# Cross-attention on one core: the context's normalisation and the batch's last body rescheduled, the last key sums inverted in 16 columns

## The chip, the core and the metric

One core of a Trainium2 chip. The metric is the device time of one execution in microseconds; lower is better. Everything is float32; products are made from a high part in `fp32r` and a low remainder, so that each product takes three matmuls (high x high, high x low, low x high).

## What is computed

Eight batches of 512 queries `x` and 512 context rows, width 1024, 16 heads of 64:

```python
a = layer_norm(ctx, gamma, beta)
Q, K, V = x @ Wq.T, a @ Wk.T, a @ Wv.T          # split into 16 heads
scores = where(mask, Q @ K.T / 8, -inf)
out = (softmax(scores) @ V) @ Wo.T
return x + tanh(gate) * out
```

## The kernel before

**Bodies.** Each batch `b` has eight bodies `j`, one for a pair of heads: 64 bodies `k = 8 b + j`. Body `k` makes the scores of pair `k`, the projections Q, K and V of pair `k + 1` (a `stream` of 72 matmuls of 512 columns, handed out in portions by `take`), the products of the probabilities with V, and the output projection of pair `k - 2`. A body's `kind` is "plain", "prepare" (`j` = 6, which also transposes the next batch's normalised context, `turn_ctx`) or "switch" (`j` = 7, whose projections are the first to read the next batch's `x` and context). The last body, 63, is written out by itself.

**Queues.** Each engine runs its own list in the order written, and semaphores join them; there is no planner. TensorE's order is `body` with the portions in `FILL`. For each head of a pair the scores go to PSUM (`sc`), VectorE takes maxima (L790, L796), ScalarE and VectorE pass them across partitions (`gather_maxima` L581, `key_maxima` L802, `hand_out_maxima` L586, `spread_maxima` L807), VectorE subtracts (L812), ScalarE does `exp` (L601) and the high part `p_high` (L606), GpSimd the low part `p_low` (L1055), and TensorE multiplies with V (`values`, L377 and L378). GpSimd also adds up the probabilities (`key_sums`, L1059 and L1061), scales the output of the pair before (`o_scale`, L1066) and makes its low part (L1070).

**Between bodies.** `copy_vt` (L591) is the first thing ScalarE does in a body. It copies the V just projected out of PSUM; the bank it frees takes the next Q projection, so that projection waits for it (`vt_done`). `q_high`, `q_low` (L612, L840), `k_high` and `k_low` (L619, L845) split the projected Q and K; the next body's scores wait for them, and the V projection, which uses Q's bank, waits for `q_low`.

**The context of the next batch** is loaded in bodies 1 to 3. VectorE takes statistics of half rows (`row_stats`, L895) in bodies 2 to 5. In body 5 it joins them (`row_moments`), ScalarE makes variance plus epsilon and the negated mean (`moments`, L629), GpSimd the reciprocal deviation (L1074) and then normalises four blocks of 128x1024 (`norm_rows`, L1078). In body 6 TensorE transposes, and ScalarE applies gamma and beta (`a_float`, L661), two blocks at a time, eight in all. At the end of body 6 ScalarE makes the high parts of the first four blocks (`a_high`, L670), at the start of body 7, behind `copy_vt`, those of the other four; GpSimd makes the low parts (`a_low`, L1089) in body 7. `x_high` (L657) and `x_low` do the same for `x` in body 6; block 0 stands before `gather_maxima`. The rows that carry the mask in the key operand are written at the end of body 7 (`mask_rows`, L638).

**The first batch** splits the weights as well: ScalarE `split_w` (L576) and GpSimd (L1050), up to four of 128x1024 in each body; SyncE loads them to `w_raw` and stores the parts in HBM (`keep_w`) for the other batches (`load_kept`).

**The last body.** The sums of exponentials come from matmuls with ones (L497, L498), which leave the same sum in all rows, 512 columns. VectorE inverts 64x512 for each head (`inverse_rows`, L957), scales the last pair's output (L949), ScalarE makes its high part `last_hi` (L645), VectorE the low part (L953). The output projections of pairs 62 (`before_pair`) and 63 (`last_pair`) are added in PSUM; VectorE adds them to `xy` (`gather`, L962), and SyncE stores.

## Time and profile before

| what | us |
|---|---|
| median of 3 runs | 2028.72 (2027.18 to 2029.65) |
| profiled execution, its own time | 2029.85 |
| its span, first to last instruction | 2028.0 |
| mean granted TensorE clock | 0.995 of full |

The page gives one line of busy times for the engines; in the timelines each line is an instruction or several alike: start, duration (of all of them together), engine, line, operation, tiles, count, and in brackets the idle time before it and what ended it. The end of a matmul is modelled, so a 512-column matmul shows about 0.39 us though the next starts 0.23 us after it; an idle time in brackets counts from the modelled end and is about 0.16 us shorter than the time that was lost.

### The profile page before, as it was taken

The page shows a single profiled execution, that of the slowest core. Times are in us where ns is not written, and L with a number is a line of the kernel's source. Part 1 is how long each engine was busy: PE and PEld are TensorE (multiplying, and loading weights), DVE is VectorE, ACT ScalarE, POOL GpSimd, SP SyncE. Part 2 cuts the span into 40 slices and gives each one's busy share as a digit, 9 for nine tenths or more (in the row PEclk, how much of TensorE's full clock was granted, in tenths as well). Part 3 has the DMA queues.
Part 4 walks back from the last instruction along what each step waited for, and adds up shares of the span by engine and source line. Part 5 has one row for each costly group of instructions (what it writes and reads, how often), then busy time and mean ns, then how long its engine had stood idle before and what let it go on. Part 6 is the DMA issues. An engine that isn't in the chain of part 4 may idle for free.

```text
span 2028.0 us, 26183 instructions
## 1 busy us (share of the span) xinstructions
PE 1957.3 (97%) x8720; PEld 1590.0 (78%) x8720; DVE 1617.7 (80%) x2074; ACT 1282.3 (63%) x2362; POOL 1501.9 (74%) x831
## 2 busy tenths in 40 slices
PE   5899989999999999999999999999999999999997
PEld 4688768888788877888778887788778888788885
DVE  6688667887778877888778887788877888787887
ACT  5767766567656585656865657665675566755563
POOL 5899996769865788667876678666886668857663
PEclk9999999999999999999999999999999999999998
DMA  6577544653355443554345553454433644434422
GB/s 243 187 249 251 181 155 158 223 185 137 126 185 194 169 167 106 211 202 144 136 149 189 189 187 108 148 211 167 167 124 135 246 157 157 146 123 174 168 93 97
DMA packets 136501, 341.95 MB, mean 169 GB/s; under 512 B 55856, under 2 KB 56880, under 8 KB 135472
## 3 DMA queue, kind: packets, MB, share of 16 engines
q1 hardware_dynamic: 136368, 340.28, 47.6%
q8 instruction: 70, 1.15, 0.2%
q14 instruction: 63, 0.52, 0.1%
HBM read 288.86 MB, written 51.36 MB: 168 GB/s over the span
## 4 chain that ended last, share of the span: by engine, by line
PE 78%; POOL 9%; ACT 5%; DVE 4%; issue 2%; DMA 2%; SPq 1%; ACTq 0%; DVEq 0%; POOLq 0%
PE pj L433 14%; PE pj L437 14%; PE pj L435 14%; PE sc L383 5%; PE sc L387 5%; PE sc L384 5%; PE sc L359 5%; PE pv L377 5%; PE sc L360 5%; PE pv L378 5%; POOL a_lo L1089 4%; POOL p_lo L1055 2%; DVE mq L790 1%; PE pj L366 1%; DMA xy<-in_xT 1%
## 5 line engine op out<-in xcount | busy, mean ns | idle before, releaser
L1055 POOL TENSOR_TENSOR p_lo<-prob,p_hi 128x1024 fp32r<-128x1024 f32 x256 | 613.5, 2407 | 185.7 <-ACT p_hi L606 185.6
L433 PE MATMUL pj<-a_hi,w_hi 128*128 128x512 f32 x1024 | 403.3, 394 | 5.9 <-DVE v_st L834 2.3
L437 PE MATMUL pj<-a_hi,w_lo 128*128 128x512 f32 x1024 | 401.2, 392 | 0.0
L435 PE MATMUL pj<-a_lo,w_hi 128*128 128x512 f32 x1024 | 400.8, 391 | 0.0
L790 DVE TRANSPOSE_TENSOR_REDUCE mq<-sc 128x32 f32<-128x1024 f32 x256 | 304.6, 1228 | 100.3 <-PE sc L360 99.3
L857 DVE SCALAR_TENSOR_TENSOR xy<-sc,tg_b,xy 128x1024 f32<-128x1024 f32 x244 | 306.1, 1273 | 44.0 <-PE sc L387 38.1
L601 ACT ACTIVATE prob<-prob 128x1024 f32<-128x1024 f32 x256 | 271.6, 1061 | 109.6 <-DVE prob L812 109.3
L812 DVE TENSOR_TENSOR prob<-sc,m_b 128x1024 f32<-128x1024 f32 x256 | 301.6, 1220 | 4.4
L1059 POOL TENSOR_TENSOR prob<-prob 128x1024 f32<-128x1024 f32 x126 | 302.4, 2400 | 0.0
L606 ACT CAST p_hi<-prob 128x1024 fp32r<-128x1024 f32 x256 | 269.4, 1052 | 3.5
L1066 POOL TENSOR_TENSOR r_b<-o,r_b 128x512 f32<-128x512 f32 x62 | 80.9, 1304 | 242.0 <-DVE r_b L829 242.0
L433 PEld LDWEIGHTS pj<-a_hi,w_hi 128*128 128x128 f32 x1024 | 193.0, 188 | 50.8 <-POOL a_lo L1089 5.1
L437 PEld LDWEIGHTS pj<-a_hi,w_lo 128*128 128x128 f32 x1024 | 193.0, 188 | 41.6
L435 PEld LDWEIGHTS pj<-a_lo,w_hi 128*128 128x128 f32 x1024 | 193.1, 189 | 41.0
L612 ACT CAST qt<-pj 64x512 fp32r<-64x512 f32 x128 | 74.4, 581 | 233.2 <-PE sc L360 208.5
L377 PE MATMUL pv<-p_hi,v_st 128*128 128x512 f32 x512 | 201.0, 393 | 19.2 <-POOL p_lo L1055 19.2
L433 PE MATMUL pj<-x_hi,w_hi 128*128 128x512 f32 x512 | 208.2, 407 | 5.7 <-issue 4.4
L359 PE MATMUL sc<-qt,kt 128*128 128x512 f32 x512 | 201.4, 393 | 12.6 <-ACT cx L661 4.9
L435 PE MATMUL pj<-x_lo,w_hi 128*128 128x512 f32 x512 | 202.2, 395 | 0.0
L437 PE MATMUL pj<-x_hi,w_lo 128*128 128x512 f32 x512 | 201.4, 393 | 0.0
L378 PE MATMUL pv<-p_lo,v_st 128*128 128x512 f32 x512 | 200.2, 391 | 0.0
L360 PE MATMUL sc<-qt,kt 128*128 128x512 f32 x512 | 200.1, 391 | 0.0
(122 smaller groups left out, 3700.2 us busy)
## 6 DMA issues: line engine op xcount, KB each, us to landing
w_hi<-kept_hi SPq DMA_DIRECT2D x225, 512.0 KB, 3.7
w_lo<-kept_lo SPq DMA_DIRECT2D x225, 512.0 KB, 4.6
cx<-in_ctx SPq DMA_DIRECT2D x32, 512.0 KB, 6.5
xy<-in_xT SPq DMA_DIRECT2D x32, 512.0 KB, 6.3
kept_hi<-w_hi SPq DMA_DIRECT2D x32, 512.0 KB, 5.3
kept_lo<-w_lo SPq DMA_DIRECT2D x32, 512.0 KB, 6.1
out_y<-xy SPq DMA_DIRECT2D x7, 2048.0 KB, 9.8
w_raw<-in_wq SPq DMA_DIRECT2D x8, 512.0 KB, 5.3
```

The costliest lines, as they stand in the source:

```text
L359: pe.matmul(sc[:, s], kt[:, h, 0, cols], qt[:, h, 0], start=True, stop=False)
L360: mm = pe.matmul(sc[:, s], kt[:, h, 1, cols], qt[:, h, 1], start=False, stop=True)
L377: pe.matmul(pv[h][:, 0], w, p_hi[:, s], start=s == 0, stop=False)
L378: mm = pe.matmul(pv[h][:, 0], w, p_lo[:, s], start=False, stop=s == TB - 1)
L433: pe.matmul(dst, w_hi[:, w, cols], s_hi[:, i], start=i == 0, stop=False)
L435: pe.matmul(dst, w_hi[:, w, cols], s_lo[:, i], start=False, stop=False)
L437: mm = pe.matmul(dst, w_lo[:, w, cols], s_hi[:, i], start=False, stop=i == KT - 1)
L790: dve.tensor_reduce(out=mq[:, 2 * i:2 * i + 2], in_=sc[:, 2 * i:2 * i + 2].rearrange("p s (b j) -> p s b j", j=32), op=ALU.max, axis=mybir ...
L812: dve.tensor_tensor(prob[:, h, 2 * i:2 * i + 2], sc[:, 2 * i:2 * i + 2], m_b[:].rearrange("p (o t) -> p o t", o=1).to_broadcast((P, 2, T)) ...
L857: dve.scalar_tensor_tensor(out=y, in0=sc[:, 2 * where:2 * where + 2], scalar=tg_b[:, bass.ds(parity, 1)], in1=y, op0=ALU.mult, op1=ALU.add ...
L1055: pool.tensor_tensor(p_lo[:, 2 * i:2 * i + 2], prob[:, h, 2 * i:2 * i + 2], f32(p_hi[:, 2 * i:2 * i + 2]), ALU.subtract).then_inc(pl_done, 1)
L1059: pool.tensor_tensor(prob[:, h, 0:2], prob[:, h, 0:2], prob[:, h, 2:4], ALU.add).then_inc(sum_done, 1)
```

## The change

- Row statistics are regrouped, and joined in two pairs: blocks 0 and 1 in body 4, blocks 2 and 3 in body 5 (`MOMENTS`). GpSimd makes the reciprocal deviations of a pair behind `key_sums(k, 0)`.
- The normalisation itself goes from GpSimd to ScalarE, in quarters of two passes each, an addition of the negated mean and a product (`norm_quarter`): behind `hand_out_maxima` of the second head in bodies 4 and 5, and before `gather_maxima` of the first head in bodies 5 and 6 (`NORM`).
- In body 6 all `x_high` of the first half stand behind `hand_out_maxima(k, 0)`. In body 7 the first four `a_high` stand behind `copy_vt` and `o_high`, the other four behind `hand_out_maxima(k, 0)`, and `mask_rows` behind `hand_out_maxima(k, 1)`.
- TensorE, body 7, second head: the nine matmuls that followed the second half of `values` now precede it (`late`).
- SyncE, body 7 of the first batch: the load of the last weight block, and the stores of the one before, stand further ahead.
- Last body: each sum is reduced with transposition to 16 columns (`row_sums`), inverted there and spread by one transposition (`last_inverse`). One `gather` moves behind the last low part, and `before_pair(1)` behind the first two `last_pair`.

The start of the kernel calls the changed helpers with b = -1 and does the same work as before. The diff, cut:

```diff
...
 CTX_LOADS = {1: (0, 1), 2: (2,), 3: (3,)}
-ROW_STATS = {(2, 1): (0,), (3, 0): (1,), (3, 1): (2,), (4, 0): (3, 4), (4, 1): (5,), (5, 0): (6, 7)}
-MASK_BODY, NORM_BODY = 2, 5
+ROW_STATS = {(2, 1): (0,), (3, 0): (1, 2), (3, 1): (3,), (4, 0): (4,), (4, 1): (5,), (5, 0): (6, 7)}
+
+MOMENTS = {(4, 0): 0, (5, 0): 1}
+NORM = {(4, 1): 0, (5, 0): 1, (5, 1): 2, (6, 0): 3}
+MASK_BODY = 2
...
                 k = PAIRS - 1
+                sp.wait_ge(wlo_done, NUMBER[WO, k - 2] + 1)
+                sp.dma_start(w_raw[:, NUMBER[WO, k - 1] % 2], wts[WO][k - 1]).then_inc(w_ld[NUMBER[WO, k - 1] % 2], 16)
                 sp.wait_ge(w_out[WV], 32 * PAIRS)
                 load_kept(WV, 0, k)
+                keep_w(NUMBER[WO, k - 2])
                 exchange_sums(k - 1)
...
                 load_kept(WK, 1, k)
-                sp.wait_ge(wlo_done, NUMBER[WO, k - 2] + 1)
-                sp.dma_start(w_raw[:, NUMBER[WO, k - 1] % 2], wts[WO][k - 1]).then_inc(w_ld[NUMBER[WO, k - 1] % 2], 16)
-                keep_w(NUMBER[WO, k - 2])
                 sp.wait_ge(wlo_done, SPLITS)
...
                         values(*before, 0)
-                    take(stream, f[1])
+                    late = f[2] if kind == "switch" and h else 0
+                    take(stream, f[1] + late)
                     if started:
...
                         turn_v(k)
-                    take(stream, f[2])
+                    take(stream, f[2] - late)
                     out_step(k, h, 0, kind)
...
                 before_pair(0, upper)
-                pe.wait_ge(pinv_done, 1)
+                pe.wait_ge(prow_done, 1)
                 before_pair(2, pj_both)
-                pe.wait_ge(acc_done, 4 * k - 4)
-                before_pair(1, lower)
                 pe.wait_ge(w_in_last, 32)
...
                 last_pair(2, pj_both)
+                pe.wait_ge(acc_done, 4 * k - 4)
+                before_pair(1, lower)
                 last_pair(1, lower)
...
-            def moments(b):
-                act.wait_ge(bn_done, b * 3 * TB + 6 * TB)
-                act.activation(vpe[:], mv[:, :, 1], ACT.Identity, bias=eps[:]).then_inc(stat_done, 1)
-                act.mul(nmean[:], mv[:, :, 0], -1.0).then_inc(stat_done, 1)
+            def moments(b, pair):
+                rows = slice(0, TB) if b < 0 else slice(2 * pair, 2 * pair + 2)
+                act.wait_ge(bn_done, b * 3 * TB + (6 * TB if b < 0 or pair else 4 * TB + 3))
+                act.activation(vpe[:, rows], mv[:, rows, 1], ACT.Identity, bias=eps[:]).then_inc(stat_done, 1)
+                act.mul(nmean[:, rows], mv[:, rows, 0], -1.0).then_inc(stat_done, 1)
+
+            def norm_quarter(b, s):
+                act.wait_ge(stat_done, b * 4 + 4 + 2 * (s // 2))
+                act.activation(cx[:, s], cx[:, s], ACT.Identity, bias=nmean[:, s:s + 1]).then_inc(centre_done, 1)
+                act.wait_ge(rstd_done, b * 2 + 2 + s // 2)
+                act.wait_ge(centre_done, b * TB + s + 1)
+                act.mul(cx[:, s], cx[:, s], rstd[:, s:s + 1]).then_inc(z_done, 1)
...
                     o_high(k - 2)
-                if kind == "prepare":
-                    x_high(k, b, 0, (b + 1) % 2)
+                if (j, 0) in NORM and b < B - 1:
+                    norm_quarter(b, NORM[j, 0])
+                if kind == "switch":
+                    for i in range(KT // 2):
+                        a_high(k, b, i)
+                gather_maxima(k, 0)
+                hand_out_maxima(k, 0)
                 if kind == "switch":
...
                         a_high(k, b, i)
-                gather_maxima(k, 0)
-                hand_out_maxima(k, 0)
                 split_w(b, WV, j + 1)
                 if kind == "prepare":
-                    for i in range(1, KT // 2):
+                    for i in range(KT // 2):
                         x_high(k, b, i, (b + 1) % 2)
...
                 q_high(k, 1)
-                if j == NORM_BODY and b < B - 1:
-                    moments(b)
+                if (j, 0) in MOMENTS and b < B - 1:
+                    moments(b, MOMENTS[j, 0])
                 gather_maxima(k, 1)
                 hand_out_maxima(k, 1)
+                if kind == "switch":
+                    mask_rows(k, b)
+                if (j, 1) in NORM and b < B - 1:
+                    norm_quarter(b, NORM[j, 1])
                 split_w(b, WQ, j + 2)
...
                     a_float(b, 7)
-                    for i in range(KT // 2):
-                        a_high(k + 1, b, i)
-                if kind == "switch":
-                    mask_rows(k, b)
                 if splits(b, WO, j - 1):
...
             act.wait_ge(eps_done, 1)
-            moments(-1)
+            moments(-1, 0)
             for i in range(KT):
...
-            def row_moments(b):
-                dve.wait_ge(bn_done, b * 3 * TB + 5 * TB)
-                dve.nop(nofuse=True)
-                for s in range(TB):
+            def row_moments(b, pair):
+                dve.wait_ge(bn_done, b * 3 * TB + (3 * TB + 2 * TB if b < 0 else 4 * TB + pair * (TB + 2)))
+                for s in range(TB) if b < 0 else (2 * pair, 2 * pair + 1):
                     dve.bn_aggr(mv[:, s], bn[:, s].rearrange("p a c -> p (a c)")).then_inc(bn_done, 1)
...
                     row_stats(b, i)
-                if stats and j == NORM_BODY:
-                    row_moments(b)
+                if stats and (j, 0) in MOMENTS:
+                    row_moments(b, MOMENTS[j, 0])
                 if stats and j == MASK_BODY:
...
-            def inverse_rows(h, sums):
+            def row_sums(h, sums):
                 dve.wait_ge(psum_done, 2 * h + 2)
-                dve.reciprocal(last_r[halves[h]], sums[halves[h]]).then_inc(pinv_done, 1)
+                dve.tensor_reduce(out=mq[:, h], in_=sums.rearrange("p (b j) -> p b j", j=32), op=ALU.max,
+                                  axis=mybir.AxisListType.X, apply_transpose=True).then_inc(prow_done, 1)
+
+            def last_inverse():
+                for h in range(2):
+                    dve.wait_ge(prow_done, h + 1)
+                    dve.reciprocal(r_inv[halves[h]], mq[halves[h], h]).then_inc(pinv_done, 1)
+                dve.wait_ge(pinv_done, 2)
+                dve.transpose(last_r.rearrange("p (b i) -> p b i", i=32),
+                              r_inv[:].rearrange("p (b o) -> p b o", o=1).to_broadcast((P, 16, 32))).then_inc(pinv_done, 1)
...
                 gather(4 * k - 5, upper, 2)
-                inverse_rows(0, pj[0])
-                gather(4 * k - 4, lower, 3)
+                row_sums(0, pj[0])
                 o_add(k, 1, last_o)
-                inverse_rows(1, pv[0][:, 0])
-                dve.wait_ge(pinv_done, 2)
+                row_sums(1, pv[0][:, 0])
+                last_inverse()
+                dve.wait_ge(pinv_done, 3)
                 dve.wait_ge(oadd_done, k * 2 + 2)
...
                 low(k, last_lo, last_r, last_hi)
+                gather(4 * k - 4, lower, 3)
                 gather(4 * k - 3, upper, 0)
...
                 row_stats(-1, i)
-            row_moments(-1)
+            row_moments(-1, 0)
             dve.wait_ge(rstd_done, 1)
...
-            def norm_rows(b, blocks=range(TB)):
-                pool.wait_ge(stat_done, b * 2 + 4)
-                pool.tensor_tensor(rstd[:], vpe[:], nhalf[:], ALU.pow).then_inc(rstd_done, 1)
-                pool.wait_ge(rstd_done, b + 2)
-                pool.nop(nofuse=True)
-                for s in blocks:
+            def deviations(b, pair):
+                rows = slice(0, TB) if b < 0 else slice(2 * pair, 2 * pair + 2)
+                pool.wait_ge(stat_done, 2 if b < 0 else b * 4 + 4 + 2 * pair)
+                pool.tensor_tensor(rstd[:, rows], vpe[:, rows], nhalf[:, rows], ALU.pow).then_inc(rstd_done, 1)
+
+            def first_norm():
+                pool.wait_ge(rstd_done, 1)
+                for s in range(2, TB):
                     pool.tensor_scalar(cx[:, s], cx[:, s], nmean[:, s:s + 1], rstd[:, s:s + 1], ALU.add,
...
                 key_sums(k, 0)
+                if (j, 0) in MOMENTS and b < B - 1:
+                    deviations(b, MOMENTS[j, 0])
                 split_w(b, WQ, j + 2)
...
                 split_w(b, WK, j + 2)
-                if j == NORM_BODY and b < B - 1:
-                    norm_rows(b)
                 if begun:
...
             split_w(0, WQ, 0)
-            norm_rows(-1, range(2, TB))
+            deviations(-1, 0)
+            first_norm()
             for i in range(KT // 2, KT):
...
```

## Rows read from the trace of the kernel before

**Rows 1.** The page, part 1: engine, busy us (share of the span) xinstructions.

```profile
PE 1957.3 (97%) x8720; PEld 1590.0 (78%) x8720; DVE 1617.7 (80%) x2074; ACT 1282.3 (63%) x2362; POOL 1501.9 (74%) x831
```

**Rows 2.** Who waited for whom, TensorE: total us, times, longest us.

```profile
PE pv L377 <- POOL p_lo L1055: 19.2, 11, 3.4
```

**Rows 3.** Timeline, ScalarE: start us, us, operation [idle before <-releaser], bodies 29 to 32.

```profile
937.47 0.59 ACT L591 COPY vt<-pj 128x512 f32<-128x512 f32 x1 [1.00 <-PE pj L437]
...
967.17 0.59 ACT L591 COPY vt<-pj 128x512 f32<-128x512 f32 x1 [1.00 <-PE pj L437]
...
1002.94 0.59 ACT L591 COPY vt<-pj 128x512 f32<-128x512 f32 x1
...
1034.11 0.59 ACT L591 COPY vt<-pj 128x512 f32<-128x512 f32 x1 [0.76 <-PE pj L437]
```

**Rows 4.** Timeline, TensorE, the switch body of the fourth batch.

```profile
1001.03 0.50 PE L359 MATMUL sc<-qt,kt 128*128 128x512 f32 x1 [0.62 <-ACT cx L661]
...
1003.62 0.47 PE L433 MATMUL pj<-x_hi,w_hi 128*128 128x512 f32 x1 [0.49 <-issue]
...
1009.91 0.50 PE L383 MATMUL sc<-o_hi,w_hi 128*128 128x512 f32 x1
...
1023.91 0.50 PE L377 MATMUL pv<-p_hi,v_st 128*128 128x512 f32 x1 [1.63 <-POOL p_lo L1055]
```

**Rows 5.** Timeline, ScalarE and VectorE, around the start of that body.

```profile
1000.87 2.17 ACT L670 CAST a_hi<-cx 128x512 fp32r<-128x512 f32 x4
...
1006.15 0.66 ACT L581 COPY m_four<-m_four 32x16 f32<-32x16 f32 x3
...
1004.67 0.27 DVE L796 TENSOR_REDUCE m_four<-mq 128x16 f32<-128x64 f32 x1
```

**Rows 6.** Timeline, GpSimd and VectorE, the same body.

```profile
1021.49 2.37 POOL L1055 TENSOR_TENSOR p_lo<-prob,p_hi 128x1024 fp32r<-128x1024 f32 x1
...
1022.23 0.69 DVE L840 TENSOR_TENSOR qt<-pj,qt 64x512 fp32r<-64x512 f32 x1
```

**Rows 7.** Timeline, ScalarE, bodies 28 and 29 (plain).

```profile
930.24 1.06 ACT L601 ACTIVATE prob<-prob 128x1024 f32<-128x1024 f32 x1 [1.14 <-DVE prob L812]
...
941.09 0.66 ACT L581 COPY m_four<-m_four 32x16 f32<-32x16 f32 x3 [2.51 <-DVE m_four L796]
```

**Rows 8.** Timeline, ScalarE, start of body 46 (sixth batch).

```profile
1461.62 0.62 ACT L657 CAST x_hi<-xy 128x512 fp32r<-128x512 f32 x1 [3.12 <-DMA xy<-in_xT]
```

**Rows 9.** Timeline, ScalarE, start of body 5 (first batch).

```profile
188.87 0.59 ACT L591 COPY vt<-pj 128x512 f32<-128x512 f32 x1
```

**Rows 10.** Timeline, GpSimd, body 5 (first batch).

```profile
216.03 4.75 POOL L1078 TENSOR_SCALAR cx<-cx,nmean,rstd 128x1024 f32<-128x1024 f32 x4 [0.18 <-POOL rstd L1074]
```

**Rows 11.** Timeline, TensorE, bodies 6, 7 and 8 (first batch).

```profile
224.49 0.65 PE L377 MATMUL pv<-p_hi,v_st 128*128 128x512 f32 x1 [3.37 <-POOL p_lo L1055]
...
285.16 0.50 PE L377 MATMUL pv<-p_hi,v_st 128*128 128x512 f32 x1 [2.60 <-POOL p_lo L1055]
...
300.10 0.47 PE L433 MATMUL pj<-x_hi,w_hi 128*128 128x512 f32 x1 [1.38 <-ACT vt L591]
```

**Rows 12.** Windows: stretch, length, busy by engine (PE first), then PEclk, DMA share, GB/s.

```profile
224.50:228.50 4.00, 4.00 (x11) 3.15 (x12) 2.42 (x5) 1.97 (x7) 4.00 (x2) 0.57 0.03 11
285.00:289.50 4.50, 4.34 (x12) 3.44 (x13) 1.17 (x4) 2.95 (x5) 4.42 (x4) 0.62 0.13 40
2014.50:2020.00 5.50, 5.44 (x13) 4.28 (x14) 1.93 (x2) 0.00 (x0) 0.00 (x0) 0.50 0.06 25
```

**Rows 13.** Timeline, VectorE and TensorE, the last body.

```profile
1997.36 0.25 DVE L826 RECIPROCAL r_inv<-r_sum 128x16 f32<-128x16 f32 x1
...
1997.65 0.71 DVE L829 STREAM_TRANSPOSE r_b<-r_inv 128x512 f32<-128x512 f32 x1
...
2004.60 3.34 DVE L957 RECIPROCAL w_raw<-pj 64x512 f32<-64x512 f32 x1
...
2014.56 0.77 PE L383 MATMUL sc<-x_hi,w_hi 128*128 128x512 f32 x1 [3.56 <-ACT x_hi L645]
```

3 lines of the change are left out of this document (2 added, 1 removed).

## The prediction

> **What bounds the kernel now.** Read the page's part 1 first: TensorE is busy 97% of the span, the other engines 63 to 80% [rows 1]. So a change here can only win back stretches in which TensorE waits or runs at half clock, and it loses wherever it makes another engine late for TensorE. The waits of TensorE come next: the longest entry is the products with V (L377) waiting for the low parts of the probabilities from GpSimd, 19.2 us [rows 2]. Then find where they lie. ScalarE copies the new V out of PSUM once in each body, as soon as TensorE has finished it, so the starts of L591 are a ruler for bodies: the plain body 29 takes 967.17 - 937.47 = 29.70 us; body 30, which also transposes the context, 35.77; body 31, the batch's last, 31.17 [rows 3]. Body 31 has a plain body's matmuls, and both of its neighbours wait, so the loss sits at the turn of each batch. Everything else that can be won is in the first batch and behind the last body's scores.
>
> **The turn of a batch, six times (batches 2 to 7).** In body 31 TensorE stops four times; each wait is the start in its row less the expected start, one matmul (0.23 us, from 29.70 us for 128 matmuls of 512 columns and a short transposition) after the one before [rows 4]:
> (a) 1001.03, 0.78 us, for the last `a_float` of ScalarE. The change does not touch the chain before it: it stays.
> (b) 1003.62, 0.64 us, for `copy_vt`, which stands behind four `a_high` (2.17 us) [rows 5]. They go behind it: the copy starts at 1000.95, is out by 1001.55, ahead of the end of the scores (1002.98). Gone.
> (c) 1009.91, 0.27 us, for the first subtraction. Four more `a_high` behind the copy, as long again, kept `gather_maxima` back until 1006.15, though VectorE's maxima were there at 1004.67 + 0.27 [rows 5]. Now only the first four lie there, 1001.95 to 1004.1. The subtraction comes 1.2 us earlier, TensorE 0.64. Gone.
> (d) 1023.91, 1.78 us, for `p_low(k, 0, 1)`, which GpSimd ended at 1023.86 after working without a break since `o_low` [rows 6]. `o_high` now runs at 1001.4 instead of 1003.4, so GpSimd starts its row 2.0 us earlier and ends it at 21.9; and `late` puts nine matmuls, 2.1 us, before these products, which TensorE reaches at 1023.91 - 1.78 - 0.91 + 2.1 = 1023.3. Gone with 1.4 us to spare.
> What is late next: the nine matmuls hold six of the V projection, which may start only when `q_low` (L840) of the second head is done, 1022.91 before [rows 6], 0.91 earlier now, so 1022.0 against TensorE at 1021.9: 0.15 us lost. `o_move(k, 0)` waits for the postponed products, so ScalarE's second half ends 0.9 us later against TensorE than in a plain body; `k_low` still ends about 0.1 us ahead of the next scores: I take nothing, at most 0.3. The mask rows (two passes, 1.5 us) fall into the wait of `o_move`, 2.3 us long, and free the end of the body. The second four `a_high` move 2.7 us later, to 1008.8; GpSimd needs the fifth at about 1012.
> Gain 0.64 + 0.27 + 1.78 - 0.15 = 2.5, and some 0.2 because the matmuls after a wait are issued slightly apart: **2.7 us, 2.2 to 3.0; times six 16.2**.
>
> **The context's normalisation on ScalarE.** A quarter is two passes over 128x1024. ScalarE's pass of that size costs 1.06 [rows 7], two dependent ones 2.1. Body 28 (quarter 0) and 29 (quarter 2) put it behind `hand_out_maxima(k, 1)`: there `o_move` (0.6) and a wait of 1.14 stand before `exp` [rows 7], which then starts 0.45 late; the chain behind it ends 1.0 us before the next V copy [rows 3], so this is covered. The wait for `rstd` costs nothing there: GpSimd makes it while the maxima are passed round. Quarter 1 lies in the gap of 2.51 us before `gather_maxima` in body 29 [rows 7], quarter 3 in the same gap of body 30, which `x_high(0)` leaves. If a pass were 1.3 us (a bias and a scale from columns), the slots overrun by up to 0.1 us each: 0 to 0.3 per batch. GpSimd's saved time in these batches is worth nothing, it has slack. Quarter 3 must be done before the transposes, 5 us later. Moving `x_high(0)` gives one thing more: in body 46 it waited 3.12 us for a transfer, with the maxima behind it [rows 8], and that body was 1.2 us longer than its like: **1.2** (0 to 1.2, as arrival varies). The row statistics are only regrouped; two in one slot were there before.
>
> **The first batch** differs, since the weights are split there as well. ScalarE has no idle time left in bodies 4 and 5: the copy of V starts at 188.87 with no wait noted [rows 9], where elsewhere it waits 1.00 for V [rows 3]. The quarter (2.1) and the wait for `rstd` behind GpSimd's sums (0.4) push `k_high` and the copy back 2.5 us; slack 0.65; TensorE loses 1.9 twice, and 0.5 where the subtraction is late: -4.3. GpSimd no longer spends 4.75 us on four normalisations [rows 10], but 1 us more on a second `rstd`, and twice waits 2.1 us for the splits: it leaves body 5 0.9 us earlier. The wait of 3.37 us at 224.49 goes [rows 11], and with it the stretch behind it with granted clock 0.57, mostly the lower level of 1.2 GHz [rows 12], eight matmuls at 0.43 instead of 0.23: +5.1. Net 0.8.
> Body 7: GpSimd works without a pause and holds TensorE. Its `a_lo` undo what (b) and (c) give, but the wait of 2.60 us [rows 11] takes in nine matmuls (2.1), and the half-clock run behind it (1.6) goes. At the end the copy of V waited for a weight split that waited for transfers: 1.38 and 0.2 of issue [rows 11]. The load of that weight and the two stores of the one before now stand ahead of the exchange of sums: gone. On SyncE the load's wait for `wlo_done` (GpSimd, 265.5) holds back the load of V's weights and all behind it by some 7 us; TensorE wants them at about 282: covered. Sum 0.8 + 2.1 + 1.6 + 1.5 = **6.0, bounds 2 and 10**.
>
> **The last body.** VectorE inverts the key sums of each head in 64x512, 3.34 us for the first [rows 13] and as much for the second, with a gather (1.2) between. The new way reduces each to 16 columns: the trace has no such pass from PSUM; bounds 0.61 (half of L790's 1228 ns) and 1.2; I take 0.70, the transposition of 128x512 being 0.71 [rows 13]. Then two inversions of 0.25, a transposition of 0.71 [rows 13], and 0.4 of semaphore steps: removed 7.9, added 2.9. The last high part and TensorE's restart move from 2014.56 to 2009.5. Before, 30 matmuls followed, the first 12 at 0.43 (granted clock 0.50 [rows 12]): 9.5 us. Now 36 follow, since `before_pair(1)` has moved behind; at full clock 36 x 0.23 + 0.3 for the low part = 8.5. **5.06 + 1.0, take 5.9**; without the full clock 3.5.
> This hangs on TensorE's wait there, now about 1.3 us instead of 3.56 [rows 13]. Here the wait of 1.63 left the clock full (the matmul took 0.50 [rows 4], those at half clock 0.65 and 0.77 [rows 11, 13]); after the one of 2.60 the granted clock fell to 0.62 [rows 12]. [...]
>
> **How the numbers follow.** 16.2 + 1.2 + 6.0 + 5.9 = 29.3 us. The profiled execution took 2029.85 (span 2028.0), less 29.3 is 2000.55; the median, 2028.72, gives **1999.4**. With all terms at their good ends it is 1993, at their bad ends 2010; as these don't meet, 1994.5 to 2006.5. Chance 0.78.
> Rival A: the first batch gives nothing, as ScalarE's extra 2.5 us per body also delays splits and loads, and the clock falls in the tail: 1999.4 + 6.0 + 2.4 = 2008. For it: ScalarE is full there; against: GpSimd's 4.75 us are surely freed. 0.12.
> Rival B: at each turn a new wait takes the place of (d), for `q_low` or `k_low`, which have 0.1 us: only (b) and (c) stay, 6 x 1.8 less: 2010. 0.06.
> Rival C, slower: a ScalarE pass with a column operand costs as much as GpSimd's p_lo, 2.37 [rows 6]. A quarter is then 4.8, 2.7 more; three slots overrun by 2.1, the fourth by 2.3, 8.6 per batch, seven batches: +60 - 29 = 2059. Break-even at 4.2 per batch, a pass of 1.8 us. Against it 1.06 in [rows 7]. By the Trainium skill, ScalarE: Activation LUTs, What ACT_TABLE_LOAD costs, such a pass is some 0.28 us + 0.833 ns per element, 1.13 us: an estimate that speaks for the forecast. The page's rules for authors want additions and products on VectorE; no run shows it here. 0.02.
> Rival D: the waits removed come back elsewhere, no change: 2028. 0.02.
> The range of 1994.5 to 2006.5 leaves the rivals out. Differences under 0.2% (4 us) can't be told from no change. Faster 0.96, same 0.02, slower 0.02.
>
> **What would show it.** Starts of L591: body 30, 35.8 before, about 33.8, since the copy starts 2 us earlier; body 31, 31.2 before, about 30.4; together 64.2 instead of 66.9. No wait before L377 in a switch body, the one before L359 unchanged. Passes on cx near 1.06 us. In the first batch new TensorE waits of about 1.9 at the ends of bodies 4 and 5, none of 3.4. In the tail the last matmul about 14 us after the first inversion starts, formerly 19. The prediction is wrong if plain bodies 4 and 5 exceed 29.8 in later batches, or if V's projection waits over 0.5 us for `q_low`.

## The result and the profile after

The changed kernel takes 2005.09 us (median of 4 runs, 2002.27 to 2006.49) against 2029.18 for the kernel before (median of 4): ratio 0.9881, 95% interval 0.9864 to 0.9898. That is 24 us faster; 1999.4 was forecast. Its profiled execution is its fastest, 2002.27 (span 2000.5); by the spans it is 27.5 us faster than the profiled one of the kernel before.

The page, part 1, after:

```profile
PE 1950.9 (98%) x8720; PEld 1585.3 (79%) x8720; DVE 1614.8 (81%) x2077; ACT 1343.3 (67%) x2432; POOL 1472.9 (74%) x810
```

TensorE executes the same 8720 matmuls and still bounds the kernel. 61 us of busy time have come to ScalarE and 29 have left GpSimd [rows 1]. The waits of TensorE after, in the form of [rows 2]:

```profile
PE sc L363 <- DVE kt L861: 7.3, 4, 2.1
PE sc L363 <- ACT cx L674: 5.0, 7, 1.2
PE pv L381 <- POOL p_lo L1080: 3.5, 3, 1.4
PE pj L437 <- POOL a_lo L1116: 2.4, 7, 0.5
```

The products with V wait 3.5 us for GpSimd instead of 19.2. In front now stand the scores behind `k_low` (two of the four waits are at the start, two at the ends of the first batch's bodies 4 and 5) and, seven times, the scores of the switch body behind the last `a_float`.

The ruler of the prediction, ScalarE's copies of V at the starts of bodies 29 to 32, as in [rows 3]:

```profile
925.17 0.59 ACT L596 COPY vt<-pj 128x512 f32<-128x512 f32 x1 [0.27 <-PE pj L441]
...
955.11 0.59 ACT L596 COPY vt<-pj 128x512 f32<-128x512 f32 x1 [0.27 <-PE pj L441]
...
988.86 0.58 ACT L596 COPY vt<-pj 128x512 f32<-128x512 f32 x1
...
1019.41 0.59 ACT L596 COPY vt<-pj 128x512 f32<-128x512 f32 x1 [0.21 <-PE pj L441]
```

Body 30 takes 33.75, body 31 30.55, together 64.30; 33.8, 30.4 and 64.2 were forecast. But body 29 takes 29.94 and not 29.70, and the idle time before the copy has shrunk from 1.00 to 0.27.

The same ruler laid over the whole span (differences of starts of the V copy; "first batch" is from the copy of body 4 to that of body 8):

| stretch | before | after | gain | forecast |
|---|---|---|---|---|
| start to body 4 | 159.17 | 157.55 | 1.6 | 0 |
| first batch, bodies 4 and 5 | 59.40 | 63.97 | -4.6 | -4.3 |
| first batch, bodies 6 and 7 | 80.80 | 69.78 | 11.0 | 10.3 |
| batches 2 to 7, bodies 6 and 7 | 402.88 | 386.57 | 16.3 | 17.4 |
| batches 2 to 7, bodies 0 to 5 | 1068.41 | 1071.20 | -2.8 | 0 |
| batch 8, bodies 56 to 62 | 207.90 | 207.98 | -0.1 | 0 |
| last body | 49.44 | 43.45 | 6.0 | 5.9 |
| sum | 2028.0 | 2000.5 | 27.5 | 29.3 |

### The profile page after: what moved, and what is told of

The parts are those of the page before. It is cut to its first block, busy times and chain, and to the rows that moved or that the text cites. A ratio compares the mean times of both kernels' runs of the same rounds, so it can differ in the third digit from the quotient of the medians.

```text
span 2000.5 us, 26247 instructions
## 1 busy us (share of the span) xinstructions
PE 1950.9 (98%) x8720; PEld 1585.3 (79%) x8720; DVE 1614.8 (81%) x2077; ACT 1343.3 (67%) x2432; POOL 1472.9 (74%) x810
## 3 DMA queue, kind: packets, MB, share of 16 engines
q8 instruction: 70, 1.15, 0.2%
## 4 chain that ended last, share of the span: by engine, by line
PE 83%; ACT 6%; DVE 6%; POOL 2%; issue 2%; DMA 1%; SPq 0%; ACTq 0%; DVEq 0%; POOLq 0%
PE pj L437 15%; PE pj L441 15%; PE pj L439 15%; PE sc L387 5%; PE sc L363 5%; PE sc L391 5%; PE sc L364 5%; PE sc L388 5%; PE pv L381 5%; PE pv L382 5%; DVE mq L806 2%; PE pj L370 1%; ACT prob L606 1%; ACT cx L674 1%; ACT x_hi L670 1%
```

## Experiments

The kernels are the changed one with one edit each, unless another base is named; segments are read with the same ruler. The kernel before took 2030.4 us beside the first four, 2029.8 beside the next four and 2029.2 beside the last three.

**The changed kernel again.** No edit.

> The changed kernel itself, looked at again. Its profiled execution spans 2000.5 us and has granted clock 0.999, while other executions took 2 to 4 us more at 0.997. Theory: these differ in how many of TensorE's waits of 2 to 2.3 us (bodies 0 to 2) and 1.3 us (last body) are followed by some eight matmuls at 0.43 instead of 0.23 us, 1.6 us for each such stretch; this profile then shows such stretches and a clock below 0.999 where its span is above 2001, and the same waits to 0.1 us. Rival: transfers arrive later in the slower executions; then the clock is 0.999 and new waits for DMA appear. Median about 2004 us, ratio to before 0.988.

Measured: 2004.79 us, ratio 0.9873 (0.9857 to 0.9889); its profiled span is 2002.3. Segment by segment it is within 0.5 us of the other profile but for one: bodies 0 to 3 take 115.34 and not 113.39. TensorE there in this run, with its window from 53 to 60 us (columns as in [rows 12]):

```profile
53.38 0.47 PE L437 MATMUL pj<-a_hi,w_hi 128*128 128x512 f32 x1 [2.04 <-DVE v_st L850]
...
54.06 0.63 PE L441 MATMUL pj<-a_hi,w_lo 128*128 128x512 f32 x1
```

The window:

```profile
53.00:60.00 7.00, 6.62 (x22) 5.31 (x23) 2.00 (x3) 3.62 (x6) 6.47 (x3) 0.76 0.75 245
```

The same in the first profile of the changed kernel:

```profile
53.44 0.47 PE L437 MATMUL pj<-a_hi,w_hi 128*128 128x512 f32 x1 [2.04 <-DVE v_st L850]
...
53.97 0.40 PE L441 MATMUL pj<-a_hi,w_lo 128*128 128x512 f32 x1
```

The window:

```profile
53.00:60.00 7.00, 6.57 (x29) 5.46 (x30) 3.56 (x5) 4.74 (x7) 6.41 (x3) 1.00 0.71 246
```

The wait is the same, 2.04 us. Behind it one execution ran eight matmuls at 0.43 us (1.2 GHz; granted clock of the window 0.76) and the other ran them at 0.23 (2.4 GHz; 1.00): 22 matmuls against 29 in the window. The DMA share is alike. So the 1.6 us that the table shows ahead of body 4 are the clock: the profile of before shows the fall, that of after does not, and the change has no part in it. All thirteen profiles of this document agree: the time to body 4 is 157.6 to 158.7 us where TensorE runs no stretch of matmuls at 0.43 ahead of it, 158.9 to 159.6 with one such stretch and 160.4 to 161.0 with two. New waits for transfers, as the rival had it, do not appear. The gain of the change itself, profile against profile, is about 26 us.

**The tail alone.** The kernel before, with `row_sums`, `last_inverse` and the new order of the last products only.

```diff
...
-                inverse_rows(0, pj[0])
-                gather(4 * k - 4, lower, 3)
+                row_sums(0, pj[0])
                 o_add(k, 1, last_o)
-                inverse_rows(1, pv[0][:, 0])
-                dve.wait_ge(pinv_done, 2)
+                row_sums(1, pv[0][:, 0])
+                last_inverse()
...
```

> The kernel before with the new last body alone (row_sums, last_inverse, the moved gather and before_pair). Theory: the time from the V copy of body 63 to the end goes from 49.4 to 43.4 us, all else stays: 6.0 us less, about 2023 us. Rival: half of it was the half-clock stretch behind the wait of 3.56 us, which the new wait of 1.3 us calls forth as well; then 3.5 us less, about 2025.5, with a stretch of 0.43 us per matmul behind the last high part.

Measured: 2025.27 us, ratio 0.9973 (0.9961 to 0.9984). The last body takes 43.36 instead of 49.44, all other segments but the start are within 0.8 us of before. TensorE, and the window behind its restart:

```profile
2010.77 0.47 PE L384 MATMUL sc<-x_hi,w_hi 128*128 128x512 f32 x1 [1.32 <-ACT x_hi L646]
```

The window:

```profile
2010.50:2016.00 5.50, 5.24 (x22) 4.13 (x23) 4.46 (x4) 0.12 (x1) 0.00 (x0) 1.00 0.22 91
```

The wait is 1.32 in place of 3.56 [rows 13], and 22 matmuls start in the 5.5 us in which 13 did [rows 12], at a granted clock of 1.00 instead of 0.50. The term of 5.9 us stands by itself: 6.1. The median is 5.1 below that of the kernel before and lies where the rival had it, but the rival needed a stretch at half clock behind the last high part, and there is none.

**The normalisation back on GpSimd.** Everything else of the change stays, the reciprocal deviations in pairs too; `norm_quarter` goes, and in body 5 GpSimd normalises the four blocks.

```diff
-                if (j, 0) in NORM and b < B - 1:
-                    norm_quarter(b, NORM[j, 0])
...
-                if (j, 1) in NORM and b < B - 1:
-                    norm_quarter(b, NORM[j, 1])
...
                 split_w(b, WK, j + 2)
+                if j == 5 and b < B - 1:
+                    norm_rows(b)
```

> The changed kernel with the four normalisations back on GpSimd in body 5, moments still in two pairs, everything else as changed. Theory: the move to ScalarE is worth little, since what GpSimd gains in the first batch (wait of 3.4 us and a half-clock stretch, 5 us) ScalarE loses there (waits of 1.68, 0.42, 1.68 and 0.44 at 188, 197, 220 and 229 us) and 0.2 to 0.4 us in each later batch: within 2.5 us of the changed kernel, bodies 4 and 5 at 29.7 us, body 6 at 40 to 42. Rival: GpSimd was the late engine and the move is the main gain outside the last body: 5 us or more slower than changed, spread over all batches.

Measured: 2004.38 us, ratio 0.9869 (0.9854 to 0.9884), span 2001.3: the change as it is gives no more. GpSimd and TensorE in the first batch:

```profile
215.30 4.80 POOL L1104 TENSOR_SCALAR cx<-cx,nmean,rstd 128x1024 f32<-128x1024 f32 x4
...
223.83 0.47 PE L381 MATMUL pv<-p_hi,v_st 128*128 128x512 f32 x1 [2.25 <-POOL p_lo L1076]
```

Bodies 4 and 5 are back at 29.73 and 29.71 (31.94 and 32.03 with the quarters), bodies 6 and 7 take 39.30 and 35.12 (36.38 and 33.40). Without the quarters the first batch wins 4.5 and loses 4.6. In the later batches body 5 is 29.70 again and not 29.94. The 39.30 of body 6 hold, behind the wait of 2.25 shown, eight matmuls at 0.43 us, 1.6 us, which another execution may lack. So the move of the normalisation, the largest part of the diff, is worth nothing in the places that the change gives it; the gain is that of the order of ScalarE's and TensorE's work at the turn, the load order and the tail.

**Without `late`.** TensorE's nine matmuls again follow the products with V.

```diff
-                    late = f[2] if kind == "switch" and h else 0
+                    late = 0
```

> The changed kernel with late = 0. Theory: in a switch body TensorE asks for p_low(k, 0, 1) at about 1009.0 and has it at 1009.85: 0.8 us lost instead of the 0.27 for q_low, so 0.5 to 0.6 us more in each of six batches, and in the first batch the wait before L381 becomes about 2.3 us, possibly with a half-clock stretch: 3 to 4 us. Total 5 to 7 us slower than changed. Rival: the postponed products delay o_move and with it k_low by as much as they save: no difference (under 1.5 us).

Measured: 2010.28 us, ratio 0.9898, by the medians 5.2 to 5.5 more than the changed kernel. The span, 2008.2, is 7.7 longer than its first profile's, but 2.9 of these lie ahead of body 4, where this execution has two stretches of matmuls at 0.43 us and that one none. The largest wait for a low part is back in body 7:

```profile
285.26 0.50 PE L381 MATMUL pv<-p_hi,v_st 128*128 128x512 f32 x1 [2.59 <-POOL p_lo L1080]
```

The first batch's body 7 is 1.3 longer (34.71), and each later batch 0.3 to 1.3. In the fourth batch the same wait reads:

```profile
1015.68 0.50 PE L381 MATMUL pv<-p_hi,v_st 128*128 128x512 f32 x1 [0.70 <-POOL p_lo L1080]
```

Here TensorE loses 0.86 of the 1.78 us of (d) [rows 4]: the earlier order on ScalarE alone removes 0.92, and `late` the rest. The next run has `late` without that order, and no wait for `p_low` in its switch bodies either, so `late` alone would have removed all of it. The wait of 2.59 at 285.26 was followed by no stretch at half clock here (granted clock 1.00 from 285 to 290), that of 2.60 before the change was [rows 12].

**`a_high` in its old places.** Four `a_high` ahead of `copy_vt` again, and the other four ahead of `gather_maxima`.

```diff
-                    for i in range(KT // 2):
+                    for i in range(KT // 2, KT):
                         a_high(k, b, i)
                 gather_maxima(k, 0)
                 hand_out_maxima(k, 0)
-                if kind == "switch":
-                    for i in range(KT // 2, KT):
-                        a_high(k, b, i)
...
                     a_float(b, 7)
+                    for i in range(KT // 2):
+                        a_high(k + 1, b, i)
```

> The changed kernel with the first four a_high back at the end of body 6 and the other four back ahead of gather_maxima; mask rows, late and the rest as changed. Theory: the waits of 0.64 (V copy) and 0.27 us (first subtraction) return in six batches, GpSimd starts o_low 2 us later and is then 1.2 us late for nothing, as late covers it: 0.9 to 1.3 us per batch, 6 to 8 us in all; in the first batch GpSimd's a_lo chain hides it. Rival: GpSimd's 2 us push p_low(k, 0, 1) past the cover of late: 2 us or more per batch, 12 us in all, with waits before L381.

Measured: 2012.18 us, ratio 0.9912, span 2010.6. ScalarE and TensorE at the turn of the fourth batch:

```profile
994.14 2.17 ACT L683 CAST a_hi<-cx 128x512 fp32r<-128x512 f32 x4
996.22 0.59 ACT L596 COPY vt<-pj 128x512 f32<-128x512 f32 x1
...
996.90 0.47 PE L437 MATMUL pj<-x_hi,w_hi 128*128 128x512 f32 x1 [0.49 <-issue]
```

The copy of V starts behind the four passes, and TensorE loses 0.65 at 996.90 and 0.25 behind it: (b) and (c) of the prediction, 0.64 and 0.27. Each later batch is 1.0 to 1.2 longer, 6.6 in six; by the medians the kernel is 7.1 to 7.8 slower. The trace names "issue" as the releaser of the first wait; the order of the rows, not the name, tells that it is the copy.

**The old load order on SyncE.** The load of the last weight block, and the stores of the one before, again behind the loads of K's weights.

```diff
-                sp.wait_ge(wlo_done, NUMBER[WO, k - 2] + 1)
-                sp.dma_start(w_raw[:, NUMBER[WO, k - 1] % 2], wts[WO][k - 1]).then_inc(w_ld[NUMBER[WO, k - 1] % 2], 16)
                 sp.wait_ge(w_out[WV], 32 * PAIRS)
                 load_kept(WV, 0, k)
-                keep_w(NUMBER[WO, k - 2])
...
                 load_kept(WK, 1, k)
+                sp.wait_ge(wlo_done, NUMBER[WO, k - 2] + 1)
...
```

> The changed kernel with SyncE's old order in body 7 of the first batch. Theory: the last weight split waits for its stores again and holds the V copy of body 8: 1.5 us more, all of it between bodies 7 and 8. Rival: with body 7 shorter by 3.7 us than before the transfers have less time, and the wait grows to 3 us or more, with a half-clock stretch.

Measured: 2007.97 us (2003.73 to 2009.09), ratio 0.9889. The profiled execution is the slowest of the four, span 2007.3. ScalarE's last weight split waits for the store of the block before; here, and then in the kernel before:

```profile
294.44 1.04 ACT L581 CAST w_hi<-w_raw 128x1024 fp32r<-128x1024 f32 x1 [3.87 <-DMA kept_lo<-w_lo]
...
298.30 1.05 ACT L576 CAST w_hi<-w_raw 128x1024 fp32r<-128x1024 f32 x1 [3.58 <-DMA kept_lo<-w_lo]
```

TensorE behind it, at the end of the first batch, and the window behind:

```profile
296.24 0.77 PE L437 MATMUL pj<-x_hi,w_hi 128*128 128x512 f32 x1 [3.61 <-ACT vt L596]
```

The window:

```profile
296.00:300.00 4.00, 3.76 (x9) 3.02 (x10) 1.85 (x3) 1.82 (x8) 4.00 (x3) 0.50 0.30 120
```

Before, the same wait of TensorE was 1.38 [rows 11]. The split starts 3.9 us earlier than before, but TensorE is there 6.1 us earlier, since body 7 has become shorter: so it waits 3.61, and then runs twelve matmuls at 0.43 us, 2.4 us more. The prediction priced this part at 1.5 us, the size of the wait in the trace of before. In this execution it is worth 6.5: 4.0 up to the V copy of body 8 and 2.5, the half clock, in the batch behind it. By the medians it is worth 2.9 to 3.6, and the fastest execution is no slower than the changed kernel's median. So the size differs between executions, and 6.5 is its upper end; the twelve slow matmuls are one part of it that can be missing. Whether the transfers land at another time was not seen, since one execution was profiled.

**The quarters in other gaps.** The quarters 0 and 2 go from behind `hand_out_maxima(k, 1)` to between `q_high(k, 0)` and `q_high(k, 1)`, where ScalarE waits for the scores of the second head; statistics and deviations half a body earlier.

```diff
+                if (j, 1) in NORM and b < B - 1:
+                    norm_quarter(b, NORM[j, 1])
                 q_high(k, 1)
...
                 hand_out_maxima(k, 1)
...
-                if (j, 1) in NORM and b < B - 1:
-                    norm_quarter(b, NORM[j, 1])
```

> The changed kernel with quarters 0 and 2 moved from behind hand_out_maxima(k, 1) into ScalarE's wait of 3.4 us between q_high(k, 0) and q_high(k, 1); for that the statistics come one step earlier, row_moments stands between group_maxima and key_maxima, moments behind hand_out_maxima(k, 0), and the reciprocal deviations before p_low(k, 0, 0). Theory: ScalarE's fullness behind the second maxima costs the first batch 1.68 + 0.42 + 1.68 + 0.44 us, and GpSimd two waits of 2 us for weight splits; all this goes, and the later batches lose less before k_low (0.1 to 0.3 us each): 5 to 8 us faster than changed, bodies 4 and 5 of the first batch at 29.7 to 30.0 us. Rival: the waits at 188 and 220 us come from the total load of ScalarE, not from the place: bodies 4 and 5 stay above 31 us.

Measured: 1998.18 us, ratio 0.9846 (0.9830 to 0.9863), span 1995.5: 6.6 us below the second run of the changed kernel, 6.2 below the next version, which ran beside it, and 5.0 by the profiles. ScalarE in body 29, and the V copy at the start of body 30:

```profile
934.88 1.16 ACT L640 ACTIVATE cx<-cx,nmean 128x1024 f32<-128x1024 f32 x1
936.12 1.15 ACT L643 ACTIVATE cx<-cx,rstd 128x1024 f32<-128x1024 f32 x1
...
938.27 0.58 ACT L617 CAST qt<-pj 64x512 fp32r<-64x512 f32 x1 [1.00 <-PE sc L364]
...
951.01 0.59 ACT L596 COPY vt<-pj 128x512 f32<-128x512 f32 x1 [0.99 <-PE pj L441]
```

Behind the quarter ScalarE still waits 1.00 for the scores, and before the V copy it waits 0.99, as before the change [rows 3]. In the first batch bodies 4 and 5 take 29.74 and 29.84, and bodies 6 and 7, with GpSimd relieved, keep their 36.35 and 33.44. Against the changed kernel that is 4.4 us in the first batch and up to 0.3 in each other. Against the version with the normalisation on GpSimd it is 4.5 in the first batch and nothing in the others (within 0.1 us each): this is what moving the normalisation can give.

**The tail's last wait filled.** Fourteen more matmuls, whose result is dropped, before the last head's scores, so that TensorE stands idle for less of its longest wait.

```diff
                 turn_v(k)
+                for _ in range(14):
+                    pe.matmul(pj[1], w_hi[:, WK, :P], x_hi[:, 5], start=True, stop=True)
                 scores(k, 1, "last")
```

> The changed kernel with 14 matmuls whose result is dropped in the last body, behind turn_v, where TensorE waits 3.4 us for the first subtraction. Theory: they end before the subtraction does, so nothing is delayed, and the eight matmuls behind the wait run at 0.23 instead of 0.43 us: 1.5 us less between the V copy of body 63 and the end. Rival: the stretch after it is bound by VectorE and GpSimd anyway, as 1.2 and 1.6 us of waits before L381 follow: no gain (under 0.4 us), these waits grow instead.

Measured: 2004.36 us, ratio 0.9873, span 2002.2. The last body takes 43.12 against 43.45 in the first profile of the changed kernel and 43.08 in the second, which had no fall of the clock there either. The own theory had 1.5 us less, the rival under 0.4; the rival held. The version with the quarters in the score wait has the stretch at 0.43 us behind this wait and takes 43.10, so the stretch costs the last body next to nothing.

**The wait for `a_float`, made in the middle of the scores.** Base: the version with the quarters in the score wait. The transposed context lies in the PSUM banks of the third and fourth block of scores, yet TensorE waited for its release ahead of the first.

```diff
-                    if kind == "switch" and h == 0:
-                        pe.wait_ge(at_done, b * KT + 2 * KT)
...
                 for i in range(2):
                     ge(pe, sub_done, k * 4 + 2 * h + i - 1)
+                    if i and floats is not None:
+                        pe.wait_ge(at_done, floats)
```

> On top of the version with the quarters in the score wait (span 1995.5, median 1998.2): in the switch bodies TensorE waits for the last a_float behind the first two blocks of the scores, whose banks hold no transposed context, not ahead of them. Own theory: wait (a) of 0.8 us (0.82 + 0.11 lost at 984.92 there) is only a matter of this order; the first half of the scores takes 0.91 us, so it goes in all seven batches: each batch of the later six 0.7 to 0.9 shorter, 5 us in all, and 0.9 in the first batch; median 1991.5 to 1993.5. Rival: the turn is held by the chain of ScalarE and GpSimd behind it (copy_vt starts only behind the last a_float, GpSimd's low parts end at the same time as before), so the 0.8 us come back within the switch body as waits for the V copy, for p_low(k, 0, 1) or for a_low: batches within 0.2 of before, median 1997 to 1998.5.

Measured: 1993.88 us, ratio 0.9825 (0.9809 to 0.9842), span 1991.3. The later batches are 0.71 to 0.83 shorter each, 4.7 together. The third block's matmul:

```profile
983.90 0.45 PE L365 MATMUL sc<-qt,kt 128*128 128x512 f32 x1
```

It starts 0.22 after the one before, with no wait; the next follows after 0.30. The own theory holds for the later batches, not for the first: body 7 takes 33.48 against 33.44. There the `a_float` comes later still. The wait of 1.36 ahead of the scores is gone, but TensorE loses 0.55 at the third block, 0.38 at the V copy and 0.25 at the first subtraction, as the rival had it; the wait for GpSimd's low part behind them is the same in both, 0.98 and 0.99.

**`q_low` ahead of `key_maxima`.** Same base; VectorE makes `q_low` of the second head while the maxima are gathered, in the switch bodies.

```diff
                 group_maxima(k, 1)
+                if kind == "switch":
+                    q_low(k, 1)
                 key_maxima(k, 1)
-                q_low(k, 1)
+                if kind != "switch":
+                    q_low(k, 1)
```

> On top of the version with the quarters in the score wait: in the switch bodies VectorE makes q_low of the second head before key_maxima, in the 0.79 us in which it waits for the gathered maxima (q_low takes 0.69). Own theory: the V projection's wait for q_low, 0.26 us in six batches and 0.6 in the batch of body 39, goes and nothing takes its place: the switch bodies 0.2 to 0.35 shorter each, median 1996 to 1997. Rival: p_low(k, 0, 1) ends at the same instant (1005.66 against q_low's 1005.67), and key_maxima comes some 0.05 later; TensorE reaches both later parts no earlier, the bodies stay within 0.1: median 1997.5 to 1998.5.

Measured: 1996.88 us, ratio 0.9838 (0.9823 to 0.9853). Its profile has a longer start (the two stretches ahead of body 4 together 2.2 more than its base), so the batches are compared: 0.2 to 0.6 shorter each, 2.3 together (0.6 in the batch of body 39, where a late step of VectorE, told of further on, is gone too); body 31 takes 30.19 instead of 30.56. The own theory holds, with 0.38 per switch body for the 0.26 expected.

**Both edits.**

> Both edits. Own theory: with TensorE 0.8 us earlier in the switch body, q_low and p_low(k, 0, 1) are the next to be late: the products with V come 1.6 us behind the low part without the edits, so 0.5 to 0.8 of it is left, and q_low ahead of key_maxima keeps the V projection free; the gains add up to 1.0 to 1.2 per later batch, median 1989.5 to 1992. Rival: they do not add, since p_low(k, 0, 1) from GpSimd is a bound that neither moves: no better than the first edit alone, within 0.5 us of it.

Measured: 1991.75 us (1990.15 to 1992.71), ratio 0.9813 (0.9799 to 0.9828), span 1988.3. VectorE in the switch body of the fourth batch:

```profile
1000.88 0.69 DVE L856 TENSOR_TENSOR qt<-pj,qt 64x512 fp32r<-64x512 f32 x1
...
1001.65 0.26 DVE L818 TENSOR_REDUCE m_all<-m_four 32x16 f32<-32x64 f32 x1
```

Body 31 takes 29.33, the later batches are 1.1 to 1.5 shorter each than in the base, 7.4 together, where the edits alone gave 4.7 and 2.3. They add up; `p_low(k, 0, 1)`, with its 1.6 us of slack, is not reached. This is the fastest version here, 37 us under the kernel before where the change gave 24.

## Why the prediction was right, and where it was not

**The turn, (a) to (d).** TensorE in the switch body of the fourth batch, after:

```profile
989.01 0.50 PE L363 MATMUL sc<-qt,kt 128*128 128x512 f32 x1 [0.63 <-ACT cx L674]
...
1009.95 0.47 PE L437 MATMUL pj<-a_hi,w_hi 128*128 128x512 f32 x1
```

and VectorE's `q_low` there:

```profile
1009.10 0.69 DVE L856 TENSOR_TENSOR qt<-pj,qt 64x512 fp32r<-64x512 f32 x1
```

(a) stays with 0.79 lost at 989.01; `copy_vt`, the subtraction and `p_low` are no longer waited for; a wait for `q_low` is new at 1009.95. All as forecast, and each tested: (b) and (c) by the old place of `a_high`, (d) by the kernel without `late`, (a) and `q_low` by the last three. Only the size of the new wait was off: 0.27 lost in five batches, where 0.15 was taken, 0.7 us over six. The start of `q_low` had been worked out to 0.1 us on either side, and that it came out so near is in part luck. In body 39 TensorE loses 0.61; the further 0.35 belong to the late step of VectorE below. The two make up the difference between 16.3 and 17.4 in the table.

Body 46, whose transfer was priced at 1.2 us: that wait is gone, and the body now exceeds its like by 0.3, which is again the late step. But the 1.2 was a matter of arrival. In the tail-only run, which has the old order, ScalarE waited 2.28 us for the same transfer and not 3.12, and the body was 0.4 longer than its like, not 1.2.

**The quarters: the step that failed.** That the later start of `exp` in bodies 28 and 29 "is covered" did not hold; the prediction's own sign for it was a plain body 4 or 5 above 29.8 in later batches, and body 5 shows 29.91 to 29.94 (30.29 in one). ScalarE and VectorE at the end of body 28, behind quarter 0, and TensorE in body 29:

```profile
915.92 1.15 ACT L640 ACTIVATE cx<-cx,nmean 128x1024 f32<-128x1024 f32 x1
917.16 1.15 ACT L643 ACTIVATE cx<-cx,rstd 128x1024 f32<-128x1024 f32 x1
...
918.69 1.05 ACT L606 ACTIVATE prob<-prob 128x1024 f32<-128x1024 f32 x1
...
923.86 0.69 DVE L861 TENSOR_TENSOR kt<-pj,kt 64x512 fp32r<-64x512 f32 x1 [0.34 <-ACT kt L625]
...
932.84 0.50 PE L387 MATMUL sc<-o_hi,w_hi 128*128 128x512 f32 x1
```

A pass with an operand per row takes 1.15 to 1.16, not the 1.06 of the passes with a constant scale, and the second starts 1.24 behind the first: the quarter holds ScalarE 2.4 and not 2.1. `exp` starts 2.8 after the handing out of the maxima instead of 2.1, late by 0.7 and not 0.45. That leaves 0.27 of ScalarE's 1.00 before the V copy, so this part is covered; but `k_low` on VectorE waits 0.34 for ScalarE, and all that VectorE does next is late by as much. Its maxima of body 29 start 1.22 behind the V copy, where they start 0.91 behind it with quarter 0 in the score wait, and TensorE, which needs the subtraction that follows, loses 0.14 and 0.11 at 932.84 and the matmul after it: 0.24 per batch, 1.4 in six. Quarter 2, in body 29, makes the next `k_low` as late (0.33), but body 30 takes 33.75 with it and without. Slack had been looked for at the V copy only; the chain that was short ran over VectorE. The range "0 to 0.3 per batch" was given, for another reason, and nothing was taken of it in the sum. The Trainium skill, ScalarE: Activation LUTs, What ACT_TABLE_LOAD costs, gave 1.13 us for such a pass. The trace agrees within 0.03 (1.15 to 1.16). The nearer row was the worse guide here, since its operand was of another kind.

**A step of VectorE that comes late, five times.** Bodies 25, 32, 39, 46 and 53, seven apart, are 0.3 to 0.4 us longer than their like in every version with the changed batches, with and without quarters, and not in the kernel before or in the tail-only one. It is one step, `key_maxima` of the second head. VectorE there in body 25 of the kernel with the quarters in the score wait (30.09), the same step of body 26 (29.68), and that of body 39 in the changed kernel:

```profile
821.98 0.25 DVE L818 TENSOR_REDUCE m_all<-m_four 32x16 f32<-32x64 f32 x1 [1.16 <-ACT m_four L586]
...
851.68 0.25 DVE L818 TENSOR_REDUCE m_all<-m_four 32x16 f32<-32x64 f32 x1 [0.79 <-ACT m_four L586]
...
1252.27 0.25 DVE L818 TENSOR_REDUCE m_all<-m_four 32x16 f32<-32x64 f32 x1 [1.14 <-ACT m_four L586]
```

ScalarE's copies, for which the step waits, begin 0.30 behind the group maxima and take 0.66 in all three, yet the step starts 0.45 to 0.47 after their end where it is late and 0.09 where it is not; in body 25 TensorE then loses 0.27 and 0.11. (In body 39 the last two versions, where `q_low` stands before this step, do not have it.) The transfers in the traces give a hint: in all 53 cases, over the eleven profiles that have them, an 8 KB transfer on one of the two queues that load instructions starts 0.64 to 0.96 us after the step, though there is only one such transfer in some 30 us. That the step is late because VectorE's instructions are loaded there is argued from this coincidence; no run tests it, and the cause stays open. Over batches 2 to 7 of the changed kernel it comes to 1.7 us. Bodies 25 and 32 hold 0.8 of the 1.2 us by which bodies 0 and 1 of the batches are longer than before; the other 0.4, about 0.1 in a first body here and there, was not traced.

**The first batch.** New waits of TensorE at the ends of bodies 4 and 5, and what is left further on:

```profile
188.37 0.47 PE L363 MATMUL sc<-qt,kt 128*128 128x512 f32 x1 [1.52 <-DVE kt L861]
...
220.40 0.47 PE L363 MATMUL sc<-qt,kt 128*128 128x512 f32 x1 [1.53 <-DVE kt L861]
...
257.12 0.50 PE L363 MATMUL sc<-qt,kt 128*128 128x512 f32 x1 [1.19 <-ACT cx L674]
...
277.64 0.47 PE L381 MATMUL pv<-p_hi,v_st 128*128 128x512 f32 x1 [0.99 <-POOL p_lo L1080]
```

1.7 lost twice (1.9 forecast), and 0.4 behind each: -4.6 for the -4.3. The 3.37 and 2.60 and the half-clock stretches behind them [rows 11, 12] are gone. Body 6 wins 6.1 where 5.1 was forecast, body 7 4.9 where 5.2 was. The net of 6.4 for 6.0 is right in part by luck: the errors have both signs, and the parts were not independent, as the load order showed. Each price was read from the trace of before, and the one for the transfer held only as long as TensorE came late.

**The last body.** VectorE, then TensorE's restart, the window behind it and the last matmul:

```profile
1983.01 0.70 DVE L972 TRANSPOSE_TENSOR_REDUCE mq<-pj 128x16 f32<-128x512 f32 x1
1983.74 0.69 DVE L868 TENSOR_TENSOR w_raw<-pv,o_tmp 64x512 f32<-64x512 f32 x1
1984.47 0.72 DVE L972 TRANSPOSE_TENSOR_REDUCE mq<-pv 128x16 f32<-128x512 f32 x1
1985.21 0.53 DVE L978 RECIPROCAL r_inv<-mq 64x16 f32<-64x16 f32 x2
1985.77 0.71 DVE L980 STREAM_TRANSPOSE w_raw<-r_inv 128x512 f32<-128x512 f32 x1
...
1988.01 0.47 PE L387 MATMUL sc<-x_hi,w_hi 128*128 128x512 f32 x1 [1.29 <-ACT x_hi L658]
```

The window:

```profile
1988.00:1994.00 6.00, 5.99 (x26) 4.71 (x27) 4.39 (x5) 0.00 (x0) 0.00 (x0) 1.00 0.32 128
```

The last matmul:

```profile
1996.25 0.39 PE L391 MATMUL sc<-x_lo,w_hi 128*128 128x512 f32 x1
```

The reductions take 0.70 and 0.72 (0.70 taken), the two inversions 0.53 (0.5), the transposition 0.71 (0.71), TensorE waits 1.29 (1.3), and the clock stays full behind it (1.00). The last matmul starts 13.2 after the first reduction does (about 14 forecast). The prediction allowed for a fall of the clock there, 2.4 us. None of the twelve profiles with the new last body shows one behind this wait (1.29 to 1.32 us). That is not the length of the wait alone. At 38 us TensorE waits 1.34 to 1.36 in every version, and in four of thirteen profiles matmuls at 0.43 us follow; without `late`, for one:

```profile
38.00:42.00 4.00, 4.00 (x12) 3.08 (x12) 0.91 (x2) 0.60 (x2) 2.05 (x1) 0.57 0.83 228
```

The granted clock is 0.57 there and 1.00 in the same stretch of the changed kernel's first profile. So the argument from the length, 1.63 without a fall and 2.60 with one, was weaker than it looked, and what decides was not found.

**The forecast of the median** was 1999.4, the median is 5.7 above it. 1.4 of these are the quarters, 0.7 `q_low`, 1.7 the late step of VectorE and 0.1 the rest of batches 2 to 7, less 0.6 by which first batch and tail did better. With its fourth run the median of the kernel before rose by 0.5. The remaining 1.9 lie between executions: the profiled execution is 2.8 below the median and lacks the fall at 54 us. The forecast treated such falls as fixed to the waits ahead of them, and they are not.

## What to carry to other kernels

When work is moved to an engine with idle time, follow the engines that wait for it as well: the V copy's 1.0 us of slack was there, `k_low`'s on VectorE was not, and the same two passes placed in a gap that ends on the bounding engine cost nothing (4.4 us faster in the first batch, up to 0.3 in each other). A wait belongs directly ahead of the instruction that touches what is waited for: moved by four matmuls it gave 0.8 us per batch, more than the largest part of the diff. And a wait for a transfer is priced by when the transfer ends against when the new kernel will get there, not by its length in the old trace, which shrinks and grows with everything ahead of it (1.4 us before; 3.6 in one execution of the new kernel with the old load order). One profile says little of such a price: four executions of that kernel lay 5.4 us apart.

## What the runs showed of the hardware

- The same wait of TensorE, 2.04 us at 53.4, was followed by a stretch at 1.2 GHz in one execution of a kernel and by none in another, and so was the tail's longest, 3.43 us. So were, from version to version, waits of 1.35 us (at 38 us, in four profiles of thirteen) and of 2.6 us (at the end of the first batch). Such a stretch is mostly six to eight matmuls at 0.43 instead of 0.23 us, 1.2 to 1.6 us, and twelve at most, 2.4 us; the profiled executions of the changed kernel and its variants carry none to three of them. Differences of up to 3.4 us ahead of body 4 between two single profiles come from this; the segments of the ruler tell where they lie.
- On ScalarE a 128x1024 pass with an operand per row takes 1.15 to 1.16 us, `exp` with a constant scale 1.05 to 1.07.
- The reciprocal deviations on GpSimd take 0.71 us for 128x2.
- VectorE's reduction with transposition of 128x512 from PSUM takes 0.70 to 0.72, no more than a transposition alone (0.71); an inversion in 64x16 takes 0.25 where one in 64x512 takes 3.34 [rows 13].
- A 32x64 reduction on VectorE started 0.45 to 0.47 us after what it waited for, and not 0.09, in five bodies of the changed kernel, seven apart, each time with an 8 KB transfer on an instruction queue 0.64 to 0.96 us behind.
